# Second layer's attention with its half-products stacked through memory, and V projected 128 tokens at a time

## What is computed

```python
    def _L1_attn_ref(x, Wq, bq, Wk, bk, Wv, bv):
        ...
        inv_scale = 1.0 / math.sqrt(hd)
        q = jnp.einsum('bse,hde->bshd', x, Wq) + bq
        k = jnp.einsum('bse,hde->bshd', x, Wk) + bk
        v = jnp.einsum('bse,hde->bshd', x, Wv) + bv
        mask = jnp.triu(jnp.full((s, s), -jnp.inf, dtype=x.dtype), k=1)
        scores = (jnp.einsum('bqhd,bkhd->bhqk', q, k) + mask) * inv_scale
        attn = jax.nn.softmax(scores, axis=-1)
        out = jnp.einsum('bhqk,bkhd->bqhd', attn, v)
        return out.reshape(b, s, h * hd)
    ...
    h = h + _L1_attn_ref(_layernorm(h, axis=-1), L1_attn_Wq, L1_attn_bq, L1_attn_Wk, L1_attn_bk, L1_attn_Wv, L1_attn_bv)
```

## Time and profile before

| | us |
|---|---|
| runs of before | 1021.05, 1022.75, 1024.42 |
| median | 1022.75 |
| the profiled execution's own time | 1024.96 |
| span of the profiled execution | 1023.2 |
| mean granted clock | 0.874 |

### The profile page before, as it was taken

How to read it: one execution, slowest core, us unless ns; L and a number is a source line. 1 busy time by engine, 2 the same in 40 slices (tenths; PEclk the granted TensorE clock), 3 DMA queues, 4 the chain that set the end, 5 groups by cost and what they waited for, 6 DMA issues and landing times.

```text
span 1023.2 us, 21497 instructions
## 1 busy us (share of the span) xinstructions
PE 804.5 (79%) x8645; PEld 616.7 (60%) x8645; DVE 670.1 (65%) x961; ACT 378.8 (37%) x550; POOL 245.3 (24%) x191
## 2 busy tenths in 40 slices
PE   4756955888996836884757788857999998999997
PEld 2434735864543524653436687645887787888885
DVE  4683786758877495687856986573567665454454
ACT  6333653540201102462153444144655642222222
POOL 5000694003899701004230111002333310000000
PEclk9976976789999967897878667778999999999999
DMA  7000000020000000000100111003444421212221
GB/s 266 1 1 1 2 1 3 2 84 0 1 0 0 1 0 1 1 1 0 55 10 3 34 34 34 2 1 100 145 153 138 157 83 57 71 59 71 59 71 48
DMA packets 20625, 44.83 MB, mean 44 GB/s; under 512 B 2448, under 2 KB 6832, under 8 KB 20176
## 3 DMA queue, kind: packets, MB, share of 16 engines
q1 hardware_dynamic: 20560, 43.89, 13.6%
HBM read 42.51 MB, written 1.36 MB: 43 GB/s over the span
## 4 chain that ended last, share of the span: by engine, by line
PE 56%; DVE 15%; ACT 3%; issue 3%; POOL 1%; DMA 1%; DVEq 0%; ACTq 0%; POOLq 0%
PE psum L1570 10%; PE psum L1569 10%; PE psum L1568 9%; PE psum L1713 5%; PE psum L1723 4%; PE psum L732 4%; PE psum L733 3%; PE psum L734 3%; PE psum L1852 2%; DVE arena L1377 1%; DVE arena L1459 1%; DVE arena L1458 1%; POOL arena L861 1%; DVE arena L1427 1%; PE psum L1762 1%
## 5 line engine op out<-in xcount | busy, mean ns | idle before, releaser
L1568 PE MATMUL psum<-xh,arena 128*128 128x296 f16 (+1 forms) x664 | 196.5, 296 | 23.2 <-DVE arena L1475 9.7
L1569 PE MATMUL psum<-xl,arena 128*128 128x296 f16 (+1 forms) x664 | 196.6, 296 | 0.0
L1570 PE MATMUL psum<-xh,arena 128*128 128x296 f16 (+1 forms) x664 | 196.2, 295 | 0.0
L1568 PE MATMUL psum<-arena 37*64 37x17 f16 (+5 forms) x1116 | 115.2, 209 | 47.6 <-DVE arena L1139 14.7
L1568 PEld LDWEIGHTS psum<-arena 37*64 37x64 f16 (+5 forms) x1116 | 92.0, 120 | 55.4 <-issue 34.4
L518 POOL TENSOR_TENSOR arena<-arena 128x768 f32 (+1 forms) x34 | 55.7, 1643 | 254.2 <-ACT arena L532 254.2
L1570 PE MATMUL psum<-arena 37*64 37x17 f16 (+5 forms) x1116 | 114.1, 206 | 2.7 <-issue 2.7
L1569 PE MATMUL psum<-arena 37*64 37x17 f16 (+5 forms) x1116 | 114.5, 206 | 2.1 <-issue 2.1
L655 DVE TENSOR_TENSOR arena<-psum,arena 128x592 f32<-128x592 f32 x64 | 49.6, 775 | 76.3 <-PE psum L1570 66.7
L732 PE MATMUL psum<-arena 128*128 (+3 forms) x340 | 92.8, 273 | 6.0 <-DVE arena L600 6.0
L1569 PEld LDWEIGHTS psum<-arena 37*64 37x64 f16 (+4 forms) x1116 | 92.8, 122 | 5.8 <-issue 2.4
(11 more groups left out here) (298 smaller groups left out, 1645.1 us busy)
## 6 DMA issues: line engine op xcount, KB each, us to landing
arena<-comb SPq DMA_DIRECT2D x64, 296.0 KB, 3.3
arena<-in_wmoe SPq DMA_DIRECT2D x34, 384.0 KB, 3.1
arena<-in_xt SPq DMA_DIRECT2D x4, 864.0 KB, 9.3
arena<-in_w SPq DMA_DIRECT2D x2, 1024.0 KB, 6.5
arena<-in_ctrl SPq DMA_DIRECT2D x1, 1056.0 KB, 9.6
out<-arena SPq DMA_DIRECT2D x2, 512.0 KB, 3.1
arena<-in_wlin SPq DMA_DIRECT2D x1, 768.0 KB, 4.5
arena<-in_wqkv SPq DMA_DIRECT2D x1, 768.0 KB, 4.1
```

The lines of the kernel that those rows point to most:

```text
L1568: pe.matmul(dst, wh, mh, start=start, stop=False)
L1569: pe.matmul(dst, wh, ml, start=False, stop=False)
L1570: return pe.matmul(dst, wl, mh, start=False, stop=stop)
```

## The change

Instead of masked copies and three matmuls for each product, the halves are stacked along the contracted rows, so that one matmul adds up all three half-products.

- Q and K. The evictions now write the high half directly with the bias (ScalarE) and the low half in one VectorE operation, tile by tile, in the order K then Q, for the first 128 features and then the second. SP stores the four half arrays of each 128 features to memory (`qk_dram`) and loads them back into `qs` and `ks`: for a pair of heads, 2 x 48 rows, which hold (high, high, low) of Q against (high, low, high) of K. `ks` is zero outside its head, which GpSimd's memset prepares. These are 12 loads for each half of the features, each of 16 rows x 4 head pairs x 1184 tokens.
- V is projected for 128 tokens at a time with the tokens as the stationary operand and 256 columns, in 5 tiles of two; its halves are stored to memory (`vv_dram`), and three loads bring (high, low, high) into `v3`, with the 37 tokens of an image in partitions 0 to 36, 37 to 73 and 74 to 110.
- Attention goes in 16 units: two halves of the heads x eight groups of four images. A unit's scores start with a matmul that writes the causal mask (identity x mask, bf16); maximum, subtraction, exponential, doubled high half (ScalarE), low half (GpSimd), 16 f16 transposes of 111 rows, copies by ScalarE and VectorE, 32 products, and the normalisation. TensorE runs scores(k), transposes(k - 2), products(k - 3).
- MoE weights: GpSimd and ScalarE split the six experts' weights inside units 3, 5, 7, 9, 11 and 13; SP issues their loads from the third on behind the transfers named above.

The products, and all scores behind them, stand after the wait for the loads of V. The diff, cut to its core:

```diff
+    for c in range(2):
+        for i in (1, 0):
             for q in range(NCH):
-                add(("qk1", i, c, q), "act")
-    for n in range(8):
+                add(("qk1", i, c, q), "dve")
+    for n in range(5):
         add(("v1", n), "dve")
...
+            for e in range(2):
+                load(wraw[:, e], a["wmoe"][0, e], f"wraw{e}")
+            for c in range(2):
+                for i, hi, lo in ((1, k1h, k1l), (0, q1h, q1l)):
+                    after(sp, ("qk1", i, c, NCH - 1))
+                    for kind, x in enumerate((hi, lo)):
+                        load(qk_dram[i, kind, 128 * c:128 * c + 128], x[:, c], f"qk_out{2 * c + i}")
+                if c == 0:
+                    sp.wait_ge(ev["pad1"], 1)
+                for i in (1, 0):
+                    sp.wait_ge(ev[f"qk_out{2 * c + i}"], 32)
+                    for x in range(2):
+                        for n, kind in enumerate((0, 1, 0) if i else (0, 0, 1)):
+                            rows = qk_dram[i, kind].rearrange("(c p x d) t -> c x d p t", c=2, p=4, x=2)[c, x]
+                            at = slice(KK * x + DH * n, KK * x + DH * n + DH)
+                            load(ks[at, 4 * c:4 * c + 4, x] if i else qs[at, 4 * c:4 * c + 4], rows, f"qs{c}")
+            after(sp, ("v1", 4))
+            for kind in range(2):
+                load(vv_dram[kind, 0:T - LAST].rearrange("(n p) e -> p n e", p=128),
+                     vt[:, kind, 0:NT - 1].rearrange("p n h v -> p n (h v)"), "vv_out")
+                load(vv_dram[kind, T - LAST:T], vt[0:LAST, kind, NT - 1].rearrange("p h v -> p (h v)"), "vv_out")
+            sp.wait_ge(ev["vv_out"], 64)
+            for n, kind in enumerate((0, 1, 0)):
+                load(v3[S * n:S * n + S].rearrange("p b h v -> p b (h v)"),
+                     vv_dram[kind].rearrange("(b s) e -> s b e", s=S), "v3")
...
+            link(pool.memset(vt[:, 0], 1.0))
+            pool.memset(vt[:, 1], 0.0).then_inc(ev["v_one"], 1)
+            pool.memset(ks, 0.0).then_inc(ev["pad1"], 1)
+            for k in range(len(UNITS)):
+                pool.wait_ge(ev["att_hi"], k + 1)
+                pool.tensor_tensor(p3[0:101, k % 3, :, 2], e_[0:101, k % 3], p3[0:101, k % 3, :, 0],
+                                   ALU.subtract).then_inc(ev["att_lo"], 1)
+                if k in LOW_AT:
+                    e = LOW_AT.index(k)
+                    pool.wait_ge(ev["wsc"], e + 1)
+                    pool.tensor_tensor(W[:, e // 2, e % 2, 1], wraw[:, e % 2], W[:, e // 2, e % 2, 0],
+                                       ALU.subtract).then_inc(ev["wlo"], 1)
...
+                        act.activation(hi[:, c, cols(q)], bank(("qk1", i, c, q))[:, 0:CH], ACT.Identity,
+                                       bias=sm(name, c)).then_inc(ev["qk1h"], 1)
...
+            for k in range(len(UNITS) + 2):
+                if k < len(UNITS):
+                    act.wait_ge(ev["att_e"], k + 1)
+                    act.activation(e_[0:101, k % 3], e_[0:101, k % 3], ACT.Exp, scale=DH ** -0.5).then_inc(ev["att_p"], 1)
+                    act.wait_ge(ev["att_p"], k + 1)
+                    if k >= 3:
+                        act.wait_ge(ev["att_t"], 2 * (k - 2))
+                    act.activation(p3[0:101, k % 3, :, 0:2], e_[0:101, k % 3].unsqueeze(2).to_broadcast([101, 16, 2, S]),
+                                   ACT.Copy).then_inc(ev["att_hi"], 1)
+                    if k in LOW_AT:
+                        e = LOW_AT.index(k)
+                        weight_high(act, e // 2, e % 2, 16 * (e // 2 + 1))
+                x = k - 2
+                if x >= 0:
+                    act.wait_ge(ev["att_t"], 2 * x + 1)
+                    if x >= 2:
+                        act.wait_ge(ev["att_o"], x - 1)
+                    act.activation(pt[0:3 * S, x % 2, 0:8], pt_bank(0), ACT.Copy).then_inc(ev["att_pa"], 1)
...
+                        dve.scalar_tensor_tensor(lo[:, c, cols(q)], bank(("qk1", i, c, q))[:, 0:CH], sm(name, c),
+                                                 hi[:, c, cols(q)], ALU.add, ALU.subtract).then_inc(emptied["dve"], 1)
...
+            for k in range(len(UNITS) + 3):
+                if k < len(UNITS):
+                    dve.wait_ge(ev["att_s"], k + 1)
+                    sc1 = s_banks(k)[0:101].rearrange("p i (h s) -> p i h s", s=S)
+                    dve.tensor_reduce(pmax[0:101, k % 2].rearrange("p (i h) -> p i h", i=2), sc1, AX, ALU.max).then_inc(ev["att_max"], 1)
+                    dve.wait_ge(ev["att_max"], k + 1)
+                    if k >= 3:
+                        dve.wait_ge(ev["att_lo"], k - 2)
+                    dve.tensor_tensor(e_[0:101, k % 3].rearrange("p (i h) s -> p i h s", i=2), sc1,
+                                      pmax[0:101, k % 2].rearrange("p (i h) -> p i h", i=2).unsqueeze(3).to_broadcast([101, 2, 8, S]),
+                                      ALU.subtract).then_inc(ev["att_e"], 1)
+                x = k - 2
+                if 0 <= x < len(UNITS):
+                    dve.wait_ge(ev["att_t"], 2 * x + 2)
+                    if x >= 2:
+                        dve.wait_ge(ev["att_o"], x - 1)
+                    dve.tensor_copy(pt[0:3 * S, x % 2, 8:16], pt_bank(1)).then_inc(ev["att_pb"], 1)
+                x = k - 3
+                if x >= 0:
+                    c, n = UNITS[x]
+                    dve.wait_ge(ev["att_o"], x + 1)
+                    link(dve.reciprocal(orec[0:101, x % 2], o_bank(x)[0:101, :, DH]))
+                    dve.tensor_tensor(o1[0:101, 2 * n:2 * n + 2, 8 * c:8 * c + 8],
+                                      o_bank(x)[0:101, :, 0:DH].rearrange("p (i h) v -> p i h v", i=2),
+                                      orec[0:101, x % 2].rearrange("p (i h) -> p i h", i=2).unsqueeze(3).to_broadcast([101, 2, 8, DH]),
+                                      ALU.mult).then_inc(ev["att_n"], 1)
...
+                for t in range(2):
+                    w = slice(128 * (2 * n + t), 128 * (2 * n + t) + 128)
+                    for k in range(2):
+                        ins = product(bk[:, D * t:D * t + D], xh[:, k, w], xl[:, k, w], wqkh[:, 2, k], wqkl[:, 2, k],
+                                      k == 0, k == 1)
...
+            def scores(k):
+                c, n = UNITS[k]
+                if n == 0:
+                    pe.wait_ge(ev[f"qs{c}"], 16 * 12)
+                if k >= 2:
+                    pe.wait_ge(ev["att_e"], k - 1)
+                for i in range(2):
+                    ps = s_banks(k)[:, i]
+                    pe.matmul(ps[0:101], identb[0:101, 0:101], causalb[0:101].unsqueeze(1).to_broadcast([101, 8, S]),
+                              start=True, stop=False, skip_group_check=True)
+                        t0, m = (4 * n + 2 * i + par) * S, (64, S)[par]
+                        for p in range(4):
+                            ins = pe.matmul(ps[64 * par:64 * par + m, 2 * S * p:2 * S * p + 2 * S],
+                                            qs[:, 4 * c + p, t0:t0 + m], ks[:, 4 * c + p, :, t0:t0 + S], start=False,
+                                            stop=True, skip_group_check=True)
+                ins.then_inc(ev["att_s"], 1)
+
+            def turn_probs(k):
+                pe.wait_ge(ev["att_lo"], k + 1)
+                if k:
+                    pe.wait_ge(ev["att_pa"], k)
+                    pe.wait_ge(ev["att_pb"], k)
+                for i in range(2):
+                    for h in range(8):
+                        ins = pe.transpose(pt_bank(i)[:, h], p3[0:101, k % 3, 8 * i + h].rearrange("p i s -> p (i s)"),
+                                           identh[0:101, 0:101])
+                    ins.then_inc(ev["att_t"], 1)
+
+            def mix(k):
+                c, n = UNITS[k]
+                if k == 0:
+                    pe.wait_ge(ev["v3"], 48)
+                pe.wait_ge(ev["att_pa"], k + 1)
+                pe.wait_ge(ev["att_pb"], k + 1)
+                if k >= 2:
+                    pe.wait_ge(ev["att_n"], k - 1)
+                for i in range(2):
+                    for bi in range(2):
+                        m = (64, S)[bi]
+                        for h in range(8):
+                            ins = pe.matmul(o_bank(k)[64 * bi:64 * bi + m, 8 * i + h],
+                                            pt[0:3 * S, k % 2, 8 * i + h, 64 * bi:64 * bi + m],
+                                            v3[:, 4 * n + 2 * i + bi, 8 * c + h], start=True, stop=True)
+                ins.then_inc(ev["att_o"], 1)
+
+            for k in range(len(UNITS) + 3):
+                if k < len(UNITS):
+                    scores(k)
+                if 0 <= k - 2 < len(UNITS):
+                    turn_probs(k - 2)
+                if k >= 3:
+                    mix(k - 3)
+            pe.wait_ge(ev["att_n"], len(UNITS))
```

248 lines of the change are left out of this document (60 added, 188 removed), and 1 row of the table EVENTS.

## The result

The changed kernel takes 1113.26 us in the median (1112.29 to 1116.54), the kernel before 1023.59 (1021.05 to 1025.66); the ratio is 1.0893, 95% interval 1.087 to 1.0917. It is 8.9% slower. The profiled execution took 1112.96 us with a span of 1111.2, against 1024.96 and 1023.2.

The account below looks back on a forecast made before the run. TensorE was taken to bound the stretch, busy 101.0 of 124.6 us. V complete at 689 plus 52 us puts turning back at 741 instead of 648.3: +92.7 on 1024.96 is 1117.7, median 1115; range 1055 to 1170.

Parts of the forecast that it names:

- rival A: V's three loads: equal shares along outer count 37 put each on one engine; 1115 us, chance 0.80.
- V's loads on one engine: 3552 packets at 33 ns in one engine's ring, 117 us (85 to 146); V complete at 689.
- the dense row: Lower bound for the price of V's packets, from the dense load: 24 ns for 544 bytes.
- the dear row: Upper bound for the price of V's packets, from the program's first load: 41 ns for 616 bytes.
- From V to the turning back: Attention after V's arrival: one product 0.9, scores 1.0, eleven units at 3.7 and tail 9.3: 52 us.
- The term for TensorE: TensorE's work per attention unit: scores 0.99, transposes 1.48, products 0.85 at 1.2 GHz; 3.3 to 3.8 us.
- The zeroing of ks: GpSimd's memset ahead of attention: 16.2 us, ending at 526.3, hidden before the first loads at 534.6.
- Projections: V as 60 matmuls in 6.4 us instead of 11.0; last eviction at 546.5, by itself 3 us won.
- Loads of Q and K: First half's twelve loads through memory, 0.42 to 1.4 us each; attention starts at 547 to 553.
- in time for unit 8 in either case: The second half's Q and K loads land at 554 to 573, before unit 8 needs them.
- Rival C: Uneven cut of V's loads, with Q and K loads at full rate too: -29 us, 994, chance 0.07.
- rival B: Uneven cut, 16 engines share V's loads: V complete at 584, -12 us, 1010, chance 0.11.

Follow-up runs that it names:

- e1_32_5: The changed kernel with each of V's three loads issued as two, of 32 rows of keys and of 5; 1040.95 us, ratio to before 1.0169.
- e2_36_1: The changed kernel with each of V's three loads issued as two, of 36 rows and of 1; 1043.95 us in a single run.
- e3_act: The changed kernel with ScalarE's weight activations moved behind the copy of the turned probabilities in six units; 1107.61 us.
- e8_nomask: e7_inter with the causal mask's two TensorE matmuls per unit left out; 1001.59 us in a single run.
- e5_groups: The changed kernel with e3_act's order, V ahead of the second half's Q and K loads, V's loads cut 32/5 and by images; 1008.75 us, ratio 0.9852.
- e7_inter: e5_groups with Q loaded into 32 partitions and V's images 24 to 31 queued behind the second half's Q and K loads; 1004.98 us, ratio 0.9838.
- e11_again: The changed kernel as it is, run again on one chip beside the kernel with the f32 view for zeroing; 1116.48 us.
- e10_best: e7_inter with ks zeroed through the f32 view; 1000.42 us, ratio to before 0.9788.

## Why the prediction was right

The forecast was 1115 and rival A; it came out at 1113.3. The mechanism was the predicted one, but the closeness is partly luck, because two terms were off by some 20 us in opposite directions.

- **V's loads on one engine.** Right, and shown by e1_32_5 and e2_36_1: TensorE waited once, at the product's line, with one engine busy. The price per packet was too high: 33 ns were taken, the middle between the dense row and the dear row, and 26.6 were measured, close to the 24 of the dense row. With a full queue the dense row was the one to take. V's stores landed at 573.3 (570 taken), V was complete at 667.8 instead of 689.
- **From V to the turning back.** 52 us were taken and 69.8 measured. This lies outside the prediction's own bounds (46 to 60), and the step failed in its form, not only in size: it compared the engines' busy times per unit and took the largest, 3.7 us. The pace is set by a loop that runs through all of them (10.26 us for two units), in which ScalarE's weight activations stood ahead of a copy that TensorE waited for; e3_act took 7.3 us out by moving them, and e8_nomask showed the loop again when TensorE lost work. In the 69.8 us TensorE is busy for 59.3: some 7 of the missing 18 us are the size of its term, some 10 are the loop. VectorE was busy for 37.6 of them, 54%, where about 90% was named as a sign. The term for TensorE was too small: the scores were put at 0.99 us, as two halves side by side, and take 1.6 (two masks of 0.42 us and two groups of eight of 0.39); the transposes 1.7 instead of 1.48, the products 1.03 instead of 0.85.
- **The zeroing of ks, "hidden, with 8 us to spare".** It was hidden from its reader, the loads into ks, and the cover named was right. What it collided with was left out: VectorE's two additions, 5.65 us on the path to the projections. In the account it is masked: the additions began 3.1 us earlier in this profile (517.1 against 520.2), and the projections themselves are 5.6 us shorter.
- **Projections.** 60 matmuls 0.11 us apart, 6.6 us (6.4 taken); TensorE's projections take 20.2 us from first to last instead of 25.8: V 4.4 less, Q and K 1.1 less (13.7 instead of 14.8). The last eviction ends at 548.1 (546.5 taken), late by the zeroing.
- **Loads of Q and K.** First scores at 552.9, inside 547 to 553; packets near the upper bound, some 300 ns against 350. The second half was in time, as long as V came late; in e5_groups to e7_inter it became a wait of its own, which the prediction's "in time for unit 8 in either case" had not seen, since there it was ahead of V in the queue.
- **Rival C and the price of an even cut.** With sixteen engines the prediction took 14 us for V's loads (5.3 to 9.1, doubled) and V complete at 584; e1_32_5, with sixteen engines by another cut, had 18.9 us and 596.9. A slowing for few partitions was right in kind, and somewhat too small. Its 1010 became 1041, since the loop's pace and the zeroing were missing there too. By its own mechanism rival B would have been slower than before, not faster.

## What to carry to other kernels

Before a transfer is written, look at its outer count: 37 rows cost 94.5 us where the same bytes as 32 and 5 rows cost 19. When several engines pass work round, add up the loop and divide by the units in flight before comparing busy times, and put work that nobody waits for behind the copy that somebody does. Work called hidden on GpSimd is only hidden if VectorE has nothing to do in that time that it can hold up; and order loads by when their first part is read, not by tensor.

## What the runs showed of the hardware

- Loads into few partitions were slow with all engines at work: into 16 partitions 132 GB/s and into 32 partitions 211 GB/s with packets of 2368 bytes, into 32 and 5 partitions 164 GB/s with packets of 544, where one engine alone moved 21 GB/s. Stores of V from 128 partitions, with the same 544 bytes, ran at 286 GB/s. The number of partitions fits all of these, but loads and stores, and loads of different sizes, were not compared with everything else alike:

```profile
...
DMA packets 1609, 0.86 MB, mean 286 GB/s; under 512 B 33, under 2 KB 1609, under 8 KB 1609
...
```

- GpSimd's zeroing of 15.88 us stopped a VectorE addition of one constant per row to an f32 tensor until it ended (6.49 us for e11_again's first addition, where two take 1.71 without it), while four two-input operations of VectorE that ran beside it just before took 3.20 us, no more than such operations take elsewhere (0.78 each). The Trainium skill (SBUF — State Buffer, "Who interferes with whom") says that operations with a scalar can enter a mode that takes the port that GpSimd shares, and then one blocks the other fully, while those with two inputs do not meet a GpSimd instruction that only writes; the trace agrees with both, since the additions stood still and the two-input operations did not.
- The zeroing takes 0.84 ns per element of a row whether the element is f16 or f32, so the f32 view halves it (15.88 and 7.99 us).
- TensorE's granted clock, 0.92 in the projections (526.3 to 547.0 us), was 0.50, 1.2 GHz, from the first scores of the changed kernel on, behind a wait of 6.2 us, to the turning back. In e7_inter it stayed there too, with TensorE busy for 8.65 of 8.79 us in two units. The kernel before had 0.68 in its first head group, and e10_best, where the wait ahead of the first scores is 2.8 us, 0.56 in the first 13.5 us. Which property of this work keeps the clock low was not tried.
- Issues are not always short: three onto one engine held SP for 59.8 us, where twelve loads of Q and K took 5.6. The MoE weights stood behind them and came late too: SP was held until 723 us with them, and ScalarE waited for one for 1.3 us, at no cost that shows behind the turning back (373.6 us against 374.9).
